# Softmax numerators divided by their sums before they are split, instead of a spread of the reciprocals by TensorE

## What is computed

```python
q, k, v = x_ln @ W_q, context @ W_k, context @ W_v          # 8 heads of 64
sim = where(mask, (q k^T) * 64**-0.5, -max)
attn = softmax(sim, axis=-1)
x = x + tanh(g_xattn) * ((attn v) @ W_o + b_o)
...
h = bitlinear(layernorm(x), w1, b1); h = gelu(h)            # 512 -> 2048
x = x + tanh(g_ffn) * bitlinear(h, w2, b2)                  # 2048 -> 512
```

## Time and profile before

| | us |
|---|---|
| median of 3 runs | 1072.77 (1072.48 to 1073.2) |
| the profiled execution, its own time | 1070.9 |
| its span, first to last instruction | 1069.1 |
| PE busy in the span | 995.9 (93%) |
| DVE, ACT, POOL busy | 835.2, 805.7, 712.1 |
| mean granted TensorE clock, of full speed | 0.99 |

### The profile page before, as it was taken

One profiled execution on the slowest core, in us unless ns is written; L12 is line 12 of the kernel. 1 busy time (PEld: TensorE's weight loads), 2 busy tenths in 40 slices (PEclk: granted clock), 3 DMA queues, 4 the chain that ended last, 5 costly groups with the idle time before them and its releaser, 6 DMA issues. The chain is left out here.

```text
span 1069.1 us, 26540 instructions
## 1 busy us (share of the span) xinstructions
PE 995.9 (93%) x9856; PEld 579.5 (54%) x9856; DVE 835.2 (78%) x1707; ACT 805.7 (75%) x1374; POOL 712.1 (67%) x691
## 2 busy tenths in 40 slices
PE   3988899999999999999999998999999999999877
PEld 2455565565555655555556555556565565555443
DVE  4788798778798777777779876788878776886976
ACT  3976787977878668796868867697786977777766
POOL 5577998577676776567576575767668666956651
PEclk9999999999999999999999999999999999999989
DMA  7989999787879979697877986988867889868750
GB/s 225 280 163 228 206 170 174 133 184 128 163 142 180 174 116 192 115 167 162 157 129 126 200 163 130 183 143 139 177 128 158 175 162 171 167 110 139 148 96 30
DMA packets 472335, 169.17 MB, mean 158 GB/s; under 512 B 450320, under 2 KB 452368, under 8 KB 471824
## 3 DMA queue, kind: packets, MB, share of 16 engines
q1 hardware_dynamic: 472208, 167.48, 80.5%
HBM read 48.28 MB, written 7.34 MB: 52 GB/s over the span
## 5 line engine op out<-in xcount | busy, mean ns | idle before, releaser
L1339 POOL TENSOR_TENSOR p<-prob,p 128x750 f16<-128x750 f32 x224 | 358.5, 1614 | 110.4 <-ACT p L1189 108.1
L1007 DVE CUSTOM_DVE_ANT_0 prob<-ps_s,mbias 128x750 f32<-128x750 f32 x224 | 204.0, 933 | 58.8 <-PE ps_s L820 47.1
L1182 ACT ACTIVATE prob<-prob,rmin 128x750 f32<-128x750 f32 x224 | 204.3, 914 | 26.2 <-DVE rmin L1007 25.8
L787 PE MATMUL ps_g<-ctx,wk 128*128 128x375 f16 x1152 | 201.8, 327 | 23.4 <-POOL ctx L1350 16.4
L787 PE MATMUL ps_g<-wv,ctx 128*128 128x512 f16 (+1 forms) x864 | 197.0, 379 | 4.1 <-DVE k_sb L1026 2.2
L787 PEld LDWEIGHTS ps_g<-ctx,wk 128*128 128x128 f16 x1152 | 111.2, 99 | 105.6 <-issue 25.7
L820 PE MATMUL ps_s<-k_sb,q_sb 64*32 64x375 f16 (+2 forms) x2688 | 128.8, 322 | 15.6 <-DVE rmin L1007 15.4
L787 PEld LDWEIGHTS ps_g<-wv,ctx 128*128 128x128 f16 (+1 forms) x864 | 86.8, 103 | 101.0 <-issue 5.9
L849 PE MATMUL ps_g<-pt,v_sb 128*64 128x224 f16 (+2 forms) x2448 | 122.8, 254 | 2.6 <-DMA pt<-p 2.4
L1189 ACT ACTIVATE p<-prob 128x750 f16<-128x750 f32 x144 | 116.0, 820 | 3.5 <-DMA pt<-p 3.0
L849 PEld LDWEIGHTS ps_g<-pt,v_sb 128*64 128x64 f16 x2448 | 109.6, 110 | 2.9 <-issue 2.8
(11 more groups left out here) (134 smaller groups left out, 1524.6 us busy)
## 6 DMA issues: line engine op xcount, KB each, us to landing
ctx_f<-in_ctx SPq DMA_DIRECT2D x47, 375.0 KB, 4.0
xa<-in_x SPq DMA_DIRECT2D x16, 448.0 KB, 4.7
xr<-in_x SPq DMA_DIRECT2D x28, 256.0 KB, 3.4
out<-xr SPq DMA_DIRECT2D x28, 256.0 KB, 2.8
pt<-p SPq DMA_TRANSPOSE x254, 4.0
h_sb<-in_w SPq DMA_DIRECT2D x4, 512.0 KB, 4.6
w<-in_w SPq DMA_DIRECT2D x3, 512.0 KB, 5.0
xr<-in_w SPq DMA_DIRECT2D x3, 512.0 KB, 5.4
```

The lines of the kernel that those rows point to most:

```text
L787: mm = nc.tensor.matmul(out, lhs, rhs, start=(m == 0), stop=(m == len(steps) - 1))
L1007: nc.vector.tensor_tensor_reduce(prob[:, (b * NU + n) % PROBS, :].rearrange("p (c k) -> p c k", c=2), ps_s[:, n % 2, :, 0:CH], mbias[:, :] ...
L1182: nc.scalar.activation(prob[:, (b * NU + n) % PROBS, :], prob[:, (b * NU + n) % PROBS, :], ACT.Exp, bias=rmin[:, n:n + 1], scale=-1.0, acc ...
L1339: nc.gpsimd.tensor_tensor(p16[:, u % HILO, 1, 0:J], prob[:, (b * NU + n) % PROBS, :], p16[:, u % HILO, 0, 0:J], ALU.subtract).then_inc(s[" ...
```

## The change

Each tile of numerators is divided by its row sums before it is split. A new step N on ScalarE multiplies the tile in place by its row's reciprocal times 512 (`RS`). H then is on GpSimd for all 14 tiles of a batch, next to L. R works on one pair of tiles at a time and gives f32 reciprocals, one small instruction per tile. The spreading matmuls, the f16 reciprocals and the f32 tile `att` go. After PV, PL on ScalarE writes the high half straight from PSUM with the scale 1/512, and PA on VectorE writes the low half straight from PSUM and frees the bank; GpSimd has no part in it. All five order lists are new; the SP list has the same 464 tokens in another order. ScalarE's list grows from 1023 to 1035 tokens, VectorE's from 1026 to 1071, GpSimd's from 580 to 656. Of the lists only a few lines are shown: a steady stretch of ScalarE's, and the head of GpSimd's.

```diff
 ACT_SEQ = in_order("""
...
-    L4:0:6 E:6:7 E:7:7 V:0:8 H:6:7 V:1:8 E:8:7 K:0:8 E:9:7 GE:0:6 PV:0:7 GS:0:6 E:10:7 V:2:8 Q:1:8 H:8:7 K:1:8
...
+    N:4:7 E:6:7 E:7:7 N:5:7 Q:0:8 Q:1:8 N:6:7 N:7:7 V:0:8 L4:0:6 E:8:7 E:9:7 N:8:7 N:9:7 V:1:8 XH:0:9 E:10:7 E:11:7
+    PL:0:7 GE:0:6 V:2:8 K:0:8 GS:0:6 V:3:8 K:1:8 E:12:7 E:13:7 L4:1:6 K:2:8 N:10:7 XH:1:9 K:3:8 K:4:8 G3:0:6 K:5:8
...
 POOL_SEQ = in_order("""
-    CX:0:0 N1:0:0 CX:1:0 CX:2:0 MB:0:0 L:0:0 L:1:0 N1:0:1 H:2:0 L:2:0 L:3:0 L:4:0 H:5:0 L:5:0 CX:0:1 CX:1:1 CX:2:1
...
+    N1:0:0 CX:0:0 CX:1:0 CX:2:0 MB:0:0 H:0:0 H:1:0 L:0:0 L:1:0 H:2:0 L:2:0 N1:0:1 H:3:0 H:4:0 L:3:0 L:4:0 H:5:0
...
 RING = 4
 EMPTIED = {
-    "O": ("x2", 1), "V": ("v_lo", 1), "F1": ("h_lin", NF), "PV": ("attn_raw", 1), "Q": ("q_lo", 1),
+    "O": ("x2", 1), "V": ("v_lo", 1), "F1": ("h_lin", NF), "PV": ("attn_lo", 2), "Q": ("q_lo", 1),
     "K": ("k_lo", 1), "F2": ("y", 1), "WM": ("w_mean", 1),
     "TX": ("xq_out", 1), "TH": ("hq_low_out", 2), "TI": ("hq_high_out", 2),
 }
@@ -345,12 +352,12 @@
     "scores": NM, "weighted": NP, "k_proj": 2 * NP, "v_proj": NT,
     "q_proj": NP,
 
-    "row_min": NU, "recips_raw": NP, "recips_hi": NP, "recips": NP, "k_lo": 2 * NP, "v_lo": NT, "q_lo": NP, "x_lo": 2, "attn_raw": NP,
+    "row_min": NU, "recips_raw": NM, "recips": NU, "k_lo": 2 * NP, "v_lo": NT, "q_lo": NP, "x_lo": 2, "attn_lo": 2 * NP,
     "x_stats": 2, "x_mean": 2, "x_cent": 2,
 
-    "expd": NU, "k_hi": 2 * NP, "v_hi": NT, "q_hi": NP, "x_hi": 2, "attn_hi": 2 * NP, "recips_out": NP, "ctx_hi": KC,
-
-    "p_lo": NU, "ctx_lo": KC, "mask_bias": 1, "x_var": 1, "x_rstd": 1, "attn_lo": 2 * NP, "w_mean": 2,
+    "expd": NU, "k_hi": 2 * NP, "v_hi": NT, "q_hi": NP, "x_hi": 2, "attn_hi": 2 * NP, "ctx_hi": KC,
+
+    "ctx_lo": KC, "mask_bias": 1, "x_var": 1, "x_rstd": 1, "w_mean": 2,
 }
 
 PER_TILE = {
@@ -458,12 +453,8 @@
         return name, (tile_of(b, n // times) - BY_PE) * times + n % times + 1
     if kind in TILED:
         return name, tile_of(b, n // times) * times + n % times + 1
-    return name, b * PER_BATCH[name] + n + 1
-
-
-
-HI_ON_ACT = [n for n in range(NU) if n not in (2, 5, 7, 10, 12)]
-HI_ON_POOL = [n for n in range(NU) if n not in HI_ON_ACT]
+    return name, b * PER_BATCH[name] + times * (n + 1)
+
 
 
 def build(nc, x_d, ctx_d, mask_d, gx_d, gf_d, wq_d, wk_d, wv_d, wo_d, bo_d, w1_d, b1_d, w2_d, b2_d, out_d):
@@ -745,7 +734,7 @@
                     sp.dma_start(xr[:, t % HELD, :], x_d[x_rows(t), :]).then_inc(d_res[t % HELD], 16)
                 elif kind == "T":
                     u = b * NU + n
-                    need(sp, "p_lo", b, n)
+                    need_lo(sp, b, n)
                     for at, size, place, after in turned_parts(b, n // 2):
                         need(sp, "weighted", 0, after)
                         sp.dma_start_transpose(pt[:, n % 2, :, place:place + size],
@@ -824,19 +813,7 @@
                     mm.then_inc(s["scores"], 1)
                 elif kind == "PV":
 
-                    need(pe, "recips", b, recips_for(b, n))
-                    j, first_query, size, row = weighs(b, n)
-                    for m in units_of(b, n):
-                        for of, q, at, many in pieces_of(b, m):
-                            if of != j or not first_query <= q < first_query + size:
-                                continue
-                            to = 256 + q - first_query
-                            for a in range(2):
-                                for e in range(2):
-                                    u = 2 * m + e
-                                    nc.tensor.matmul(g[e * DH:(e + 1) * DH, to:to + many],
-                                                     rrec16[:, a, u:u + 1].to_broadcast([128, DH]),
-                                                     ident[:, at:at + many], start=(a == 0), stop=(a == 1))
+                    j, _, size, row = weighs(b, n)
                     for m in units_of(b, n):
                         for e in range(2):
                             need_turned(pe, b * NU + 2 * m + e)
@@ -936,21 +913,15 @@
         def _(dve):
             dve.memset(half_neg[:, :], -0.5).then_inc(consts, 1)
 
-            def take_reciprocals(b, n):
-
-
-                of = recips_units(b, n)
-                need(dve, "expd", b, of.stop - 1)
-                last = pieces_of(b - 1, (of.stop - 1) // 2)[-1][0] if b > 0 else 0
-                need(dve, "weighted", b - 1, last)
-                nc.vector.reciprocal(rrec[:, of], rsum[:, of]).then_inc(s["recips_raw"], 1)
-                need(dve, "recips_raw", b, n)
-                nc.vector.tensor_scalar(rrec16[:, 0, of], rrec[:, of], RS, None, ALU.mult)\
-                    .then_inc(s["recips_hi"], 1)
-                need(dve, "recips_hi", b, n)
-                nc.vector.scalar_tensor_tensor(out=rrec16[:, 1, of], in0=rrec[:, of], scalar=RS,
-                                               in1=rrec16[:, 0, of], op0=ALU.mult, op1=ALU.subtract)\
-                    .then_inc(s["recips"], 1)
+            def take_reciprocals(b, m):
+
+                need(dve, "expd", b, 2 * m + 1)
+                need_lo(dve, b - 1, 2 * m + 1)
+                nc.vector.reciprocal(rrec[:, 2 * m:2 * m + 2], rsum[:, 2 * m:2 * m + 2]).then_inc(s["recips_raw"], 1)
+                need(dve, "recips_raw", b, m)
+                for u in (2 * m, 2 * m + 1):
+                    nc.vector.tensor_scalar(rrec[:, u:u + 1], rrec[:, u:u + 1], RS, None, ALU.mult)\
+                        .then_inc(s["recips"], 1)
 
             def emit(kind, n, b):
                 if kind == "PW":
@@ -1003,7 +974,7 @@
 
                     need(dve, "scores", b, n // 2)
                     need(dve, "mask_bias", b, 0)
-                    need(dve, "p_lo", b, n - PROBS)
+                    need_lo(dve, b, n - PROBS)
                     nc.vector.tensor_tensor_reduce(
                         prob[:, (b * NU + n) % PROBS, :].rearrange("p (c k) -> p c k", c=2), ps_s[:, n % 2, :, 0:CH],
                         mbias[:, :].rearrange("p (c k) -> p c k", c=2), 1.0, 3e38, ALU.add, ALU.min,
@@ -1011,10 +982,13 @@
                 elif kind == "R":
                     take_reciprocals(b, n)
                 elif kind == "PA":
-                    need(dve, "recips_out", b, n)
-                    qs = slice(0, queries_of(b, n))
-                    nc.vector.tensor_tensor(att[:, qs], g[:, qs], att[:, qs], ALU.mult)\
-                        .then_inc(s["attn_raw"], 1)
+                    pieces = attn_pieces(b, n)
+                    need(dve, "attn_hi", b, 2 * n + 1)
+                    for at, to, size in pieces:
+                        nc.vector.scalar_tensor_tensor(out=attn[:, 1, n % NP, to:to + size], in0=g[:, at:at + size],
+                                                       scalar=1.0 / RS, in1=attn[:, 0, n % NP, to:to + size],
+                                                       op0=ALU.mult, op1=ALU.subtract)\
+                            .then_inc(s["attn_lo"], 2 // len(pieces))
                 elif kind == "VL":
                     need(dve, "v_hi", b, n)
                     nc.vector.scalar_tensor_tensor(out=v_sb[0:KEYS[n], p, n, 1, :], in0=g[0:KEYS[n], :],
@@ -1175,31 +1149,24 @@
                 if kind in ("PD", "BD", "WB", "WL", "WQ", "WM"):
                     return
                 p = b % 2
-                g = bank(kind, n, b) if kind in EMPTIED else None
+                filled = {"PL": "PV"}.get(kind, kind)
+                g = bank(filled, n, b) if filled in EMPTIED else None
                 if kind == "E":
 
                     need(act, "row_min", b, n)
                     nc.scalar.activation(prob[:, (b * NU + n) % PROBS, :], prob[:, (b * NU + n) % PROBS, :], ACT.Exp, bias=rmin[:, n:n + 1],
                                          scale=-1.0, accum_out=rsum[:, n:n + 1]).then_inc(s["expd"], 1)
-                elif kind == "H" and n in HI_ON_ACT:
-
-                    u = b * NU + n
-                    need(act, "expd", b, n)
-                    need_turned(act, u - HILO)
-                    nc.scalar.activation(p16[:, u % HILO, 0, 0:J], prob[:, (b * NU + n) % PROBS, :], ACT.Copy)\
-                        .then_inc(hi_act, 1)
-                elif kind == "PV":
+                elif kind == "N":
+                    held = prob[:, (b * NU + n) % PROBS, :]
+                    need(act, "recips", b, n)
+                    nc.scalar.activation(held, held, ACT.Copy, scale=rrec[:, n:n + 1]).then_inc(normed, 1)
+                elif kind == "PL":
                     need(act, "weighted", b, n)
-                    need(act, "attn_lo", b, 2 * n - 1)
-                    nc.scalar.activation(att[:, 0:queries_of(b, n)], g[:, 256:256 + queries_of(b, n)], ACT.Copy, scale=1.0 / RS)\
-                        .then_inc(s["recips_out"], 1)
-                elif kind == "PL":
-                    need(act, "attn_raw", b, n)
```

(32 more changed lines are left out.)

490 lines of the change are left out of this document (245 added, 245 removed).

## The result

The changed kernel takes **1029.34 us** (median of 4 runs, 1028.07 to 1031.5), beside 1072.62 us for the kernel before on the same chip: ratio 0.9598, 95% interval 0.958 to 0.9617, 43.3 us less. I had forecast 12 us less and a range that ended at 1045. The profiled execution took 1028.6 us, with a span of 1026.7 us.

The account below looks back on a forecast made before the run. PE's stream of matmuls was taken as the bound over four fifths of the run. The terms -18.5 - 3.5 + 6 + 4 gave -12 us, from 1072.8 to 1061 us, with a range of 1045 to 1081.

Parts of the forecast that it names:

- term 2: PE's waits for reciprocals, attention low halves and row minima behind slow reciprocal passes shrink: -3.5 us, ends 0 and -7.
- terms 3 and 4: Denser engines and each tile's longer chain cost +6 us; the start, with GpSimd's longer queue, costs +4 us.
- Term 1: PE loses all 640 spreading matmuls, priced by their weight loads: -18.5 us, with 14 and 26.6 us as ends.
- Rival D: On PE, each removed spreading matmul was worth more than its load: 1034 us; chance 0.03.
- The tail: At the kernel's end, the last tiles' chain is 2 to 4 us longer but covered; nothing more counted.
- Rival A: PE's stream closes up entirely, density costs nothing and waits go in full: 1048 us; chance 0.20.
- Rival C: Five `prob` slots and ScalarE's list bind, N standing behind GELU blocks: 1085 us, 1076 to 1095; chance 0.15.
- Rival B: The saving is absorbed by PE waits of its size: 1066 to 1076 us, centre 1072; chance 0.12.

Follow-up runs that it names:

- b_recips_free: Kernel before, both reciprocal passes one column at a time, low halves with the high half as per-partition scalar; 1050.96 us, ratio 0.9799.
- b_free_no_spread: b_recips_free without the 640 spreading matmuls and PE's wait for reciprocals, ScalarE's copy writing a constant; 1044.79 us, ratio 0.9728.
- b_free_short: b_free_no_spread with the products evacuated as in the changed kernel, old lists, division left out of the output; 1032.88 us, ratio 0.9617.
- a_recips_by_pair: Changed kernel with the reciprocals scaled in one pass over two columns instead of two passes over one; 1044.67 us, ratio 0.9742.
- a_recips_two_inputs: Changed kernel with the one-column scaling of reciprocals made a pass with two SBUF tensor inputs; 1044.37 us, ratio 0.9745.
- a_spread_back: Changed kernel with 640 spreading matmuls of the same shapes put back on PE, output unread; 1036.78 us, ratio 0.9672.
- b_recips_by_column: Kernel before with both reciprocal passes one column at a time, the low-half pass keeping two SBUF inputs; 1083.7 us, ratio 1.0108.
- a_xn_odd: Changed kernel with VectorE's centring of x cut into passes of 511 columns and one column; 1031.25 us, ratio 0.9607.

## Why the prediction was wrong, point by point

The steps from the kernel before to the changed one, from the ratios, times 1072.6 us. The intervals of two ratios leave each step 2 to 3 us either way:

| step | forecast | measured |
|---|---|---|
| hold-ups of the reciprocals' passes (b_recips_free) | within term 2, -3.5 | -21.6 |
| spreading off PE (b_free_no_spread) | -18.5 | -7.6 |
| shorter evacuation of the products (b_free_short) | within term 2 | -11.9 |
| the division, GpSimd's halves and the new orders (the changed kernel) | +10 (terms 3 and 4) | -2.0 |

- **The step that failed first is term 2.** It had the mechanism in its rows and the wrong size. I took the two slow passes of the earlier trace rows as one event, counted only what PE's waits name, at most 7 us, and halved it. But a pass that is held up delays everything behind it on VectorE, and PE's wait bears the name of whatever came last. The groups show more: 67 passes each of L951 and L948 took 74 us. At the 160 to 170 ns of their shortest they would take 22, so 52 us of VectorE were held up. b_recips_free, whose passes take 53 us with none held up, gave back 21.6.
- **The rule was read, and given no price.** Of the rule that I took from the Trainium skill, "GPSIMD Engine Reference", Specifications, I wrote that by it the passes "would lose in proportion, a tenth more of today's excess; no price here hangs on it". Proportion was my reading and wrong: a pass of a shape that waits does so until the pass of GpSimd that runs is over, and the change takes away the shapes that wait. That the new shape doesn't show the hold-up I had said; I had it at 214 ns, and it took 149. L1137, from which I took 214, reads a per-partition scalar that L923 does not; L953 in b_recips_free, which reads one too, took 210.
- **Term 1** was right for PE's busy time (-18.6) and wrong for the time: 12 ns for each matmul put back, and 7.6 us for taking all of them off (with PE's wait for the reciprocals, 1.3 us by name in b_recips_free), under both my ends, 14 and 26.6 us. Where PE waits now and then, work taken off it partly becomes waiting. Rival D was wrong: the 81 ns of the Trainium skill, "TensorE: Matmul & The Clock Gate", Back-to-back issue gap, have no support in any run for these short matmuls.
- **The tail** I gave to term 2 as the 2.5 us that PE waited for L1345. The shorter evacuation was worth 11.9 us, and not in the tail: from the last row-minimum pass to the end the two kernels take 51.9 and 52.0 us.
- **Terms 3 and 4** were costs that, in sum, didn't come. Together with the orders they make -2.0 us, not told from 0. A slot of `prob` is held for 17.9 us in the mean, from the start of M to the end of L, where it was 15.4: 2.5 us more, not 4. VectorE waited 13.0 us for the slot of `prob` after, 11.2 before, so the five slots held, with ScalarE at 84%. Rival A came nearest in kind, the stream closed up, but its 1048 us had the waits at 7.
- **Rival C** had a right neighbour: N does wait for L923, 29.3 us in all. No stop of PE bears its name, and PE is idle for only 4.6 us from 200 to 960.
- **Rival B** was mis-added: the sum plus 14 is 1075 us, not the 1072 given as its centre. Its waits did not come either.

What stays open: how the 2.0 us split between the division's cost and the orders' gain, and which part of the shorter evacuation saves the 11.9. b_free_short has the old lists, so 41 of the 43 us need no new orders while the division is left out; whether the division comes as cheaply in any list but the new ones no run shows.

## What to carry to other kernels

Look for VectorE passes whose mean is a multiple of their shortest, and lay them beside GpSimd's timeline: if they end where its passes end, a pass with one SBUF input over a single column, or a per-partition scalar in place of the second input, frees them at the cost of more instructions. Price such hold-ups by VectorE's excess, as an upper bound, and not by the waits that bear their name: here 52 us of excess were worth 21.6 us (b_recips_free), 38 us 15.4 (a_recips_by_pair) and 50 us 15.8 (a_recips_two_inputs). And where the engine that bounds still has short stops, count work taken off it at less than its busy time; here, by the profiled spans, at 6.9 of 15.7 us taken off (b_free_no_spread against b_recips_free) and 8.1 of 14.7 us put back (a_spread_back).

## What the runs showed of the hardware that I had not expected

- A one-column VectorE pass with one SBUF input never waited for GpSimd (224 passes, at most 156 ns; 448 in b_recips_free, at most 219), a two-column one did in 64 of 112 and took up to 2676 ns.
- With two SBUF inputs even one column waits: 68 of 224 passes in a_recips_two_inputs (371 ns in the mean) and 56 of 224 in b_recips_by_column.
- A small pass of VectorE that is held up gets in at the end of the pass of GpSimd in which it began (67 of 68 before, 54 of 56 in b_recips_by_column), mostly even where GpSimd's next pass follows without a gap. Once it sat through nine passes, 8265 ns.
- A pass over 511 or 512 columns that is held up ends 0.28 to 0.29 us after the pass of GpSimd (26 of 26 in the changed kernel, 25 of 25 in a_xn_odd).
- A per-partition scalar in SBUF does not count as an input, over one column: 203 to 219 ns throughout (L953 in b_recips_free).
